# One order for all engines of an attention and soft-mixture layer: projections in pairs, contexts grouped, slot means in halves

## The chip, the cores and the metric

The kernel runs on one NeuronCore of a Trainium2 chip. The metric is the device time in microseconds (us) of one launch, the median over repeated runs. TensorE (PE) multiplies matrices, VectorE (DVE), ScalarE (ACT) and GpSimd (POOL) work on vectors, SyncE (SP) issues the transfers. Every engine works through its own list of instructions in order and waits on semaphores for the others.

## The reference

For each of 16 rows of the batch (256 tokens of 128 channels), with `xn = layernorm(x)`:

```
qkv = xn @ Wqkv + bqkv                      # 16 heads of 8 channels
proj = (q or k, each head scaled to length 1) @ omega   # 2 nodes x 32 features
feat = exp(clip(proj * sqrt(2s) - s, -20, 20)) / sqrt(32) * sqrt(weight)
attn = (causal sum of qf.kf * v) / (causal sum of qf.kf)
logits = rms_norm(xn) @ rms_norm(slots).T   # 512 slots
slots_in = softmax over experts of logits, applied to the tokens
hid = gelu(slots_in @ w1);  proc = hid @ w2
out = x + attn @ Wout + bout + softmax over slots of logits @ proc
```

## The kernel before, in words

**Tiling.** One row of the batch is one pass of `row(b, first, nxt, nxt2)`, and each engine has such a function with eight slots `s`. Slot `s` is built around `scores(b, s)`: the feature products of two heads (12 small matmuls, L925) into the PSUM tile `p_s`. DVE masks one half of it into `s_sb` (`evac_a`, L694), ACT copies the other (`evac_b`, L496), POOL masks that one (`mask_b`, L433). `run_rows` gives two rows out, a loop of two rows a turn, and two rows out.

**Features.** `project(b, g)` (L912) multiplies the turned stack of normalised q and k by omega, into `p_f` and `p_g`, each one bank; `clip(b, p)` (L688) moves one of them to `arg`, and `feature_exp(b, p)` (L491) makes `feat` for `scores(b, p)`. Four buffers of `arg` and of `feat` are there. `project(b, g)` waits for the clips of `g - 1`.

**The stack.** q and k of the next row (b1) pass through `qkv_product`, `qkv_bias`, `squares` (POOL, L404), `qk_norms`, `qk_root`, `qk_newton`, `qk_apply` (POOL, L419), `stack_high` (ACT, L484), `stack_low` (POOL, L427), and `turn_stack`, a transposing transfer from SP (L312) into `stack_t`. In `p_s` also stand the sums of `context` (L943).

**The slots.** Two logit products, their maxima (L720, L726), `shift`, the exponentials, `slot_sums` (L1012) into `x01`, `slots_norm` (a reciprocal and a product on DVE, L733 and L736), `slots_transposed` (L1021), `slots_high` and `slots_low`, two halves of `hidden` (L887), `gelu` (L523), two halves of `processed` (the product with w2, L1040), `proc_copy`, `combine` (L1051). What follows the hidden product of a row is done in slots 0 to 2 of the next row (bp is the row before).

**What sets the order.** It is written out by hand: the place of each call in the four `row` functions is the place of its instructions in the queue of that engine. The semaphores only hold an instruction back. `hold` is a wait with an empty instruction behind it.

Of the kernel before, what the change touches and what calls it, by code (L numbers as in the profile page):

```python
# [29 lines left out]
LN_EXP = "natural_log_exp_and_others"  # L30

# [53 lines left out]
def build(nc, x, Wqkv, bqkv, Wout, bout, omega, nodes, weights, gamma_x, gamma_slot, slot_embeds,  # L85
          w1, w2, out):
    with ExitStack() as ctx:
# [140 lines left out]
        stlo_ok = sem("stlo_ok")  # L228
        d_st = sem("d_st")
# [63 lines left out]
        def _(sp):  # L293
# [13 lines left out]
            def turn_stack(b):  # L307
                hold(sp, sthi_ok, count(b, 1, 1))
                hold(sp, stlo_ok, count(b, 1, 1))
                hold(sp, ft_ok, count(b, 4, -4))  # L310
# [53 lines left out]
        def _(pool):  # L364
# [70 lines left out]
            pool.wait_ge(d_bo, 16)  # L435
            residual((0, 0))
# [3 lines left out]
            place_v((0, 0))  # L440

# [18 lines left out]
        def _(act):  # L460
# [91 lines left out]
            ln_root(b1)  # L552
# [6 lines left out]
            stack_high(b0)  # L559
            act.wait_ge(se_cl, 1)  # L560
# [6 lines left out]
            feature_exp(b0, 0)  # L567

            def row(b, first, nxt, nxt2):

                b1, b2, bp = step(b, 1), step(b, 2), step(b, -1)
                for s in range(8):
                    if s == 0:
                        if not first:
                            ctx_copy(bp, 1)
                        feature_exp(b, 1)
                        if not first:
                            proc_copy(bp)
# [16 lines left out]
                    if s == 0 and nxt:  # L595
                        xt_high(b1)
                    if s == 4 and nxt:
                        stack_high(b1)
                    if s == 5 and nxt2:
                        ln_root(b2)  # L600
                    if s == 7:
# [3 lines left out]
                        if nxt:  # L605
                            feature_exp(b1, 0)
# [9 lines left out]
        def _(dve):  # L616
# [23 lines left out]
            def ln_apply(b):  # L640
# [3 lines left out]
                after(dve, sl_ok, count(b, 1, -1))  # L644
# [512 lines left out]
```

## Time and profile before

| | us |
|---|---|
| median of 3 runs (573.86 to 579.02) | 576.27 |
| the profiled execution | 578.53 |
| its span in the trace | 576.5 |
| PE busy | 484.0 (84%) |
| DVE busy | 348.8 (61%) |
| ACT busy | 322.6 (56%) |
| POOL busy | 174.1 (30%) |

A span is the time from the first to the last instruction in the trace; 2.0 us of the profiled execution lie outside it. Busy times of different engines overlap. An idle time stands in front of an instruction with the engine and the line that ended it.

### The profile page before, as it was taken

To read this page: it belongs to the slowest core of one execution; us is meant where nothing else is said; L and a number is where in the kernel's file an instruction comes from. 1 tells how busy PE (TensorE), PEld (TensorE's weight loads), DVE (VectorE), ACT (ScalarE), POOL (GpSimd) and SP (SyncE) were. 2 spreads that over 40 slices of the span, in tenths; PEclk is the share of its full clock that TensorE was granted. 3 is DMA by queue.
4 is the path that set the end of the run, shared out by engine and by line. 5 is a ranking of instruction groups with operands and counts; after the bars stand their busy time and mean duration, and the time that the engine had idled before them with its cause. 6 is when DMAs were issued, how large, how long until landed. Compare 5 with 4: busy or idle time off the path is not lost.

```text
span 576.5 us, 16010 instructions
## 1 busy us (share of the span) xinstructions
PE 484.0 (84%) x5768; PEld 394.3 (68%) x5768; DVE 348.8 (61%) x889; ACT 322.6 (56%) x560; POOL 174.1 (30%) x278
## 2 busy tenths in 40 slices
PE   4077998889799898979989897998989798898986
PEld 2056777768687676867767686776768677776866
DVE  3667484954748376574848647394775739484451
ACT  3237557455665647575564656656475655746562
POOL 4324141422414133231413324141332414233120
PEclk9999899979999799999989899898999989998999
DMA  2312002020200202020020202002020200102000
GB/s 71 75 24 48 1 11 47 10 48 2 53 5 9 45 9 45 0 55 0 9 45 9 45 0 50 5 9 45 9 45 0 55 0 9 38 11 38 3 9 9
DMA packets 45779, 14.46 MB, mean 25 GB/s; under 512 B 35640, under 2 KB 45624, under 8 KB 45752
## 3 DMA queue, kind: packets, MB, share of 16 engines
q1 hardware_dynamic: 45000, 13.80, 11.3%
q10 hardware_dynamic: 752, 0.30, 0.2%
q8 instruction: 17, 0.28, 0.2%
q14 instruction: 10, 0.08, 0.0%
HBM read 3.61 MB, written 2.10 MB: 10 GB/s over the span
## 4 chain that ended last, share of the span: by engine, by line
PE 53%; DMA 13%; DVE 13%; issue 9%; ACT 4%; POOL 4%; SPq 2%; DVEq 1%; POOLq 0%; ACTq 0%
PE x L887 15%; DMA stack_t<-stack 12%; PE x L1040 10%; PE p_s L925 9%; PE x L1051 5%; PE p_s L943 4%; DVE arg L688 4%; POOL stack L427 3%; DVE maxima L720 3%; PE p_f L912 2%; ACT stack L484 2%; DVE maxima L726 2%; PE x L966 2%; DVE small L672 2%; PE x L954 2%
## 5 line engine op out<-in xcount | busy, mean ns | idle before, releaser
L433 POOL TENSOR_TENSOR s_sb<-s_sb,causal 128x256 f32<-128x256 f32 x128 | 93.7, 732 | 306.9 <-ACT s_sb L496 306.9
L694 DVE TENSOR_TENSOR s_sb<-p_s,causal 128x384 f32<-128x384 f32 x128 | 70.6, 552 | 122.9 <-PE p_s L925 122.5
L925 PE MATMUL p_s<-feat 64*64 64x256 f32 (+3 forms) x2048 | 104.7, 322 | 10.3 <-ACT feat L491 6.2
L925 PEld LDWEIGHTS p_s<-feat 64*64 64x64 f32 x2048 | 82.8, 139 | 42.8 <-issue 33.4
L496 ACT ACTIVATE s_sb<-p_s 128x384 f32<-128x384 f32 x128 | 62.8, 490 | 85.2 <-PE p_s L925 84.9
L491 ACT ACTIVATE feat<-arg,f_bias 128x512 f32<-128x512 f32 x128 | 91.3, 714 | 0.2
L688 DVE TENSOR_SCALAR arg<-p_f,f_low,f_high 128x512 f32<-128x512 f32 x64 | 51.6, 806 | 26.1 <-PE p_f L912 26.1
L1040 PE MATMUL x<-w_sb,hid_t 128*128 128x128 f32 x512 | 64.0, 278 | 0.0
L1040 PEld LDWEIGHTS x<-w_sb,hid_t 128*128 128x128 f32 x512 | 60.8, 192 | 4.6 <-issue 3.2
L912 PE MATMUL p_f<-stack_t,omega_st 64*128 64x512 f16 x64 | 25.7, 402 | 41.4 <-DMA stack_t<-stack 41.4
L523 ACT ACTIVATE hid_t<-x 128x1024 f32<-128x1024 f32 x32 | 32.8, 1024 | 45.8 <-PE x L887 45.8
L943 PE MATMUL p_s<-s_sb,vw 128*32 128x128 f32 x1536 | 48.6, 274 | 6.7 <-DVE s_sb L694 6.7
L688 DVE TENSOR_SCALAR arg<-p_g,f_low,f_high 128x512 f32<-128x512 f32 x64 | 51.3, 801 | 0.0
L943 PEld LDWEIGHTS p_s<-s_sb,vw 128*32 128x32 f32 x1536 | 40.2, 110 | 13.1 <-DVE s_sb L694 11.2
L912 PEld LDWEIGHTS p_f<-stack_t,omega_st 64*128 64x128 f16 x64 | 6.0, 93 | 49.6 <-issue 46.4
L887 PE MATMUL x<-slot_hi,w_hi 128*128 128x512 f32 x64 | 34.0, 531 | 0.3 <-DVE slot_lo L741 0.3
L1012 PE MATMUL x<-xg,disp 128*128 128x129 f32 x256 | 32.8, 281 | 0.0
L1012 PEld LDWEIGHTS x<-xg,disp 128*128 128x128 f32 x256 | 29.8, 191 | 3.2 <-issue 3.2
L1051 PE MATMUL x<-proc,comb_t 128*128 128x129 f32 x256 | 31.4, 275 | 0.2 <-ACT proc L528 0.2
L1051 PEld LDWEIGHTS x<-proc,comb_t 128*128 128x128 f32 x256 | 30.7, 191 | 0.6 <-ACT proc L528 0.5
L887 PE MATMUL x<-slot_hi,w_lo 128*128 128x512 f32 x64 | 30.4, 476 | 0.0
L887 PE MATMUL x<-slot_lo,w_hi 128*128 128x512 f32 x64 | 30.3, 473 | 0.0
(131 smaller groups left out, 838.9 us busy)
## 6 DMA issues: line engine op xcount, KB each, us to landing
xin<-in_L_attn_x_dram SPq DMA_DIRECT2D x32, 64.0 KB, 2.4
out_dram<-out_sb SPq DMA_DIRECT2D x32, 64.0 KB, 2.1
se_rows<-n_L_ffn_slot_embeds_dram SPq DMA_DIRECT2D x1, 256.0 KB, 5.1
w_f<-in_L_ffn_w_dram SPq DMA_DIRECT2D x1, 256.0 KB, 5.3
w_sb<-in_L_ffn_w_dram SPq DMA_DIRECT2D x1, 256.0 KB, 4.7
stack_t<-stack SPq DMA_TRANSPOSE x16, 4.4
bqkv_bc<-in_L_attn_bqkv_dram ACTq DMA_DIRECT2D x1, 192.0 KB, 5.0
wqkv_f<-in_L_attn_Wqkv_dram SPq DMA_DIRECT2D x1, 192.0 KB, 4.9
```

Source lines behind the costliest of these rows:

```text
L433: pool.tensor_tensor(v, v, m, ALU.mult).then_inc(mb_ok, 1)
L491: nc.scalar.activation(feat[:, p % 4, :], arg[:, p % 4, :], ACT.Exp, bias=f_bias[:, 0:1]).then_inc(fe_ok, 1)
L496: nc.scalar.activation(s_sb[:, p, 1, :], p_s[:, 1, 0:384], ACT.Copy).then_inc(eb_ok, 1)
L688: nc.vector.tensor_scalar(arg[:, p % 4, :], bank[:, :], f_low[:, 0:1], f_high[:, 0:1], ALU.max, ALU.min).then_inc(cl_ok, 1)
L694: nc.vector.tensor_tensor(s_sb[:, p, 0, :], p_s[:, 0, 0:384], causal[:, :], ALU.mult).then_inc(ea_ok, 1)
L887: mm = nc.tensor.matmul(dst, a, w, start=start and i == 0, stop=stop and i == 2, skip_group_check=True)
L912: nc.tensor.matmul(bank[:, :], omega_st[rows, g, :], stack_t[rows, b[1], :, :, g, :].rearrange("p j k t -> p k j t"), start=True, stop=Tru ...
L925: mm = nc.tensor.matmul(p_s[rows:rows + 64, u, o:o + hi - lo], f[:, T + keys:T + keys + 64], f[:, lo:hi], start=True, stop=True, skip_grou ...
L943: mm = nc.tensor.matmul(p_s[32 * q:32 * q + 32, j, 384:512], vw[:, b[1], kt, QUADS * a + q, :], s_sb[:, p, q % 2, o:o + 128], start=(kt == ...
L1012: mm = nc.tensor.matmul(x01[:, half, 129 * (c % 2):129 * (c % 2) + 129], disp[:, j, 128 * c:128 * c + 128], xg[:, b[1], j, :], start=(j == ...
L1040: mm = nc.tensor.matmul(x01[:, 1, 128 * c:128 * c + 128], hid_t[:, m, 128 * c:128 * c + 128], w2_sb[:, m, :], start=(m == 0 and c == 0), s ...
L1051: mm = nc.tensor.matmul(x23[:, 0, 129 * j:129 * j + 129], comb_t[:, c, 128 * j:128 * j + 128], proc[:, c, :], start=(c == 0), stop=(c == N ...
```

## The change

The arithmetic stays; the order of calls on four engines changes, and three calls are split or moved.

- PE: `project(b, 0)` stands at the end of the row before, behind `scores(bp, 7)`, no longer ahead of the hidden products; `project(b, 1)` and `project(b, 2)` stand around the last contexts, ahead of `scores(b, 0)`. `project(b, 3)` is in slot 3 ahead of `shift`. `context(b, 0)` and `(b, 1)` go from slot 4 to slot 5, behind `slots_transposed`, both hidden products one slot forward.
- DVE: the clips follow the projections, so `clip(b, 4)` stands ahead of `evac_a(b, 0)` and three of them at the row's start; `ln_stats(b2)` moves from slot 4 to slot 0. `slots_norm` is two calls of half the size. `stack_again` is a new copy, float16 from SBUF to SBUF, of the part of the stack that ACT wrote twice before.
- ACT: one copy fewer in `stack_high`; the exponentials follow the clips; the table of the Gelu is loaded behind `ctx_copy(b, 0)`, no longer when the Gelu comes.
- SP: `turn_stack` also waits for the new copy.
- Before the rows: POOL's `residual((0, 0))`, with its wait for the bias, goes behind the work on the first stack; `project(b0, 0)` goes behind the transposes of the slot embeddings; the split of w1 on DVE goes into slot 1 of row 0.

Cut to its core:

```diff
@@ -432,12 +435,12 @@
 
-            pool.wait_ge(d_bo, 16)
-            residual((0, 0))
             squares((0, 0))
             qk_apply((0, 0))
             stack_low((0, 0))
             place_v((0, 0))
+            pool.wait_ge(d_bo, 16)
+            residual((0, 0))
@@ -480,9 +483,7 @@
                 after(act, d_st, count(b, 16, 0))
-                for q in (0, 2):
-                    last = nc.scalar.activation(stacked(q), parted(), ACT.Copy)
-                last.then_inc(sthi_ok, 1)
+                nc.scalar.activation(stacked(0), parted(), ACT.Copy).then_inc(sthi_ok, 1)
@@ -564,16 +565,19 @@
                 for s in range(8):
                     if s == 0:
+                        if nxt:
+                            xt_high(b1)
+                        feature_exp(b, 0)
                         if not first:
                             ctx_copy(bp, 1)
                         feature_exp(b, 1)
+                        feature_exp(b, 2)
                         if not first:
                             proc_copy(bp)
                     if s == 2 and not first:
@@ -582,28 +586,27 @@
                         qk_root(b1)
                     if s == 4:
                         dispatch_exp(b)
+                    evac_b(b, s)
+                    if s < 3:
+                        feature_exp(b, s + 3)
+                    if s == 1 and nxt2:
+                        ln_root(b2)
+                    if s == 4:
+                        if nxt:
+                            stack_high(b1)
+                        combine_exp(b)
+                        feature_exp(b, 6)
                     if s == 5:
+                        slots_high(b)
+                        feature_exp(b, 7)
                         ctx_copy(b, 0)
-                        combine_exp(b)
+                        nc.scalar.preload_act_table_set(GELU)
                     if s == 6:
-                        slots_high(b)
-                    if s == 7:
                         gelu(b, 0)
-                    evac_b(b, s)
-                    if 0 < s < 7:
-                        feature_exp(b, s + 1)
-                    if s == 0 and nxt:
-                        xt_high(b1)
-                    if s == 4 and nxt:
-                        stack_high(b1)
-                    if s == 5 and nxt2:
-                        ln_root(b2)
                     if s == 7:
                         gelu(b, 1)
                         if nxt:
                             nc.scalar.preload_act_table_set(LN_EXP)
-                        if nxt:
-                            feature_exp(b1, 0)
 
@@ -727,13 +730,17 @@
-            def slots_norm(b):
-                after(dve, sl_ok, count(b, 1, 1))
-                v = x01[:, :, 0:258].rearrange("p a (c d) -> p a c d", d=129)
-                nc.vector.reciprocal(slot_rs[:, :, :], v[:, :, :, C]).then_inc(slr_ok, 1)
-                after(dve, slr_ok, count(b, 1, 1))
-                rs = slot_rs[:, :, :].rearrange("p a (c d) -> p a c d", d=1).broadcast_to([128, 2, 2, C])
-                nc.vector.tensor_tensor(slot_v[:, :, :].rearrange("p (a c) d -> p a c d", a=2), v[:, :, :, 0:C], rs,
+            def stack_again(b):
+                after(dve, sthi_ok, count(b, 1, 1))
+                nc.vector.tensor_copy(stacked(2), stacked(0)).then_inc(stcp_ok, 1)
+
+            def slots_norm(b, half):
+                after(dve, sl_ok, count(b, 2, half + 1))
+                v = x01[:, half, 0:258].rearrange("p (c d) -> p c d", d=129)
+                nc.vector.reciprocal(slot_rs[:, half, :], v[:, :, C]).then_inc(slr_ok, 1)
+                after(dve, slr_ok, count(b, 2, half + 1))
+                rs = slot_rs[:, half, :].rearrange("p (c d) -> p c d", d=1).broadcast_to([128, 2, C])
+                nc.vector.tensor_tensor(slot_v[:, 2 * half:2 * half + 2, :], v[:, :, 0:C], rs,
                                         ALU.mult).then_inc(slv_ok, 1)
@@ -917,8 +934,8 @@
                 hold(pe, eb_ok, count(b, 8, p))
-                if p in (0, 5):
-                    hold(pe, cs_ok, count(b, 2, p // 5))
+                if p in (0, 6):
+                    hold(pe, cs_ok, count(b, 2, p // 6))
@@ -1061,31 +1077,36 @@
             qkv_product(b0)
-            pe.wait_ge(om_s, 3)
-            project(b0, 0)
             pe.wait_ge(se_ok, 1)
             pe.wait_ge(qkvs_ok, 1)
             for c in range(NCH):
                 mm = nc.tensor.transpose(x01[:, 0, 128 * c:128 * c + 128], se_n[:, c, :], ident[:, :])
             mm.then_inc(se_t, 1)
+            pe.wait_ge(om_s, 3)
+            project(b0, 0)
             pe.wait_ge(vz_const, 2)
             pe.wait_ge(se_l, 1)
 
             def row(b, first, nxt, nxt2):
                 b1, bp = step(b, 1), step(b, -1)
                 for s in range(8):
-                    if s == 0 and not first:
-                        processed(bp, 0)
-                        context(bp, 2)
-                        context(bp, 3)
-                        processed(bp, 1)
-                    scores(b, s)
                     if s == 0:
                         if not first:
-                            ctx_transposed(bp)
+                            processed(bp, 0)
                         if nxt:
                             transposes(b1)
                         project(b, 1)
+                        if not first:
+                            context(bp, 2)
+                            context(bp, 3)
+                            processed(bp, 1)
+                            project(b, 2)
+                    scores(b, s)
+                    if s == 0:
+                        if first:
+                            project(b, 2)
+                        else:
+                            ctx_transposed(bp)
                     if s == 1:
                         if nxt:
                             qkv_product(b1)
@@ -1098,25 +1119,23 @@
                             pe.wait_ge(d_late, 16 * LATE)
                         else:
                             attention_out(bp)
-                        project(b, 2)
                         logits_tokens(b, nxt)
                         logits_slots(b)
                     if s == 3:
+                        project(b, 3)
                         shift(b)
                     if s == 4:
-                        project(b, 3)
-                        context(b, 0)
-                        context(b, 1)
                         slot_sums(b, 0)
                         slot_sums(b, 1)
                     if s == 5:
                         slots_transposed(b)
+                        context(b, 0)
+                        context(b, 1)
+                        hidden(b, nxt, 0)
                     if s == 6:
-                        if nxt:
-                            project(b1, 0)
-                        hidden(b, nxt, 0)
-                    if s == 7:
                         hidden(b, nxt, 1)
+                    if s == 7 and nxt:
+                        project(b1, 0)
 
             run_rows(pe, row)
             last_row = (B // 2 - 1, 1)
```

The new `row` of DVE (its old one is above):

```
def row(b, first, nxt, nxt2):
    b1, b2, bp = step(b, 1), step(b, 2), step(b, -1)
    for s in range(8):
        if s == 0:
            clip(b, 2)
            if nxt:
                xt_low(b1)
            clip(b, 3)
            if not first:
                if nxt2:
                    ln_stats(b2)
                clip(b, 4)
        if s == 2 and not first:
            add_experts(bp)
        if s == 3:
            token_maxima(b)
            slot_maxima(b)
        evac_a(b, s)
        if s == 0:
            if first:
                clip(b, 4)
                ln_stats(b2)
            clip(b, 5)
        if s == 1:
            if first:
...
            else:
                ctx_norm(bp)
            if nxt:
                qkv_bias(b1)
        if s == 2:
            if not first:
                add_attention(bp)
            if nxt:
                qk_norms(b1)
        if s == 3 and nxt:
            qk_newton(b1)
        if s == 4:
            clip(b, 6)
            slots_norm(b, 0)
            if nxt:
                stack_again(b1)
            slots_norm(b, 1)
        if s == 5:
            clip(b, 7)
            slots_low(b)
        if s == 6 and nxt2:
            ln_apply(b2)
        if s == 7 and nxt:
            clip(b1, 0)
            clip(b1, 1)
```

Three places of the order. First PE, from the last scores of one row to the first scores of the next. In the kernel before (`w_sb,hid_t` is `processed`, `s_sb,vw` is `context`, `ident,xg` the transposes of the next row's input):

```order
L1040 MATMUL x<-w_sb,hid_t 128x128 x8
L943 MATMUL p_s<-s_sb,vw 32x128 x24
L1040 MATMUL x<-w_sb,hid_t 128x128 x8
L925 MATMUL p_s<-feat 64x256 x2
L925 MATMUL p_s<-feat 64x192 x2
L925 MATMUL p_s<-feat 64x64 x2
L925 MATMUL p_s<-feat 64x128 x2
L954 MATMUL x<-ident,ctx_sb 128x128 x4
L895 MATMUL x<-ident,xg 128x128 x2
L912 MATMUL p_f<-stack_t,omega_st 128x512
L912 MATMUL p_g<-stack_t,omega_st 128x512
```

And in the changed kernel:

```order
L929 MATMUL p_f<-stack_t,omega_st 128x512
L929 MATMUL p_g<-stack_t,omega_st 128x512
L1056 MATMUL x<-w_sb,hid_t 128x128 x8
L912 MATMUL x<-ident,xg 128x128 x2
L929 MATMUL p_f<-stack_t,omega_st 128x512
L929 MATMUL p_g<-stack_t,omega_st 128x512
L960 MATMUL p_s<-s_sb,vw 32x128 x24
L1056 MATMUL x<-w_sb,hid_t 128x128 x8
L929 MATMUL p_f<-stack_t,omega_st 128x512
L929 MATMUL p_g<-stack_t,omega_st 128x512
L942 MATMUL p_s<-feat 64x256 x2
```

Three pairs of projections now stand between the two scores, where one pair stood behind the first scores.

Second PE, from the transposes of the slot means to the hidden product. Before:

```order
L1021 MATMUL x<-ident,slot_v 128x128 x4
L925 MATMUL p_s<-feat 64x256 x2
L925 MATMUL p_s<-feat 64x192 x2
L925 MATMUL p_s<-feat 64x64 x2
L925 MATMUL p_s<-feat 64x128 x2
L912 MATMUL p_f<-stack_t,omega_st 128x512
L912 MATMUL p_g<-stack_t,omega_st 128x512
L887 MATMUL x<-slot_hi,w_hi 128x512
```

Changed:

```order
L1037 MATMUL x<-ident,slot_v 128x128 x4
L960 MATMUL p_s<-s_sb,vw 32x128 x24
L904 MATMUL x<-slot_hi,w_hi 128x512
L904 MATMUL x<-slot_lo,w_hi 128x512
L904 MATMUL x<-slot_hi,w_lo 128x512
```

The next row's projection is gone from here, and the contexts have come in.

Third DVE, slots 4 and 5. Before:

```order
L694 TENSOR_TENSOR s_sb<-p_s,causal 128x384
L688 TENSOR_SCALAR arg<-p_f,f_low,f_high 128x512
L630 BN_STATS bn<-xin 128x6 x2
L634 BN_AGGR mv<-bn 128x2 x2
L637 TENSOR_SCALAR small<-mv 128x2
L638 TENSOR_SCALAR small<-mv 128x2
L688 TENSOR_SCALAR arg<-p_g,f_low,f_high 128x512
L733 RECIPROCAL slot_rs<-x 128x4
L736 TENSOR_TENSOR slot_v<-x,slot_rs 128x512
L694 TENSOR_TENSOR s_sb<-p_s,causal 128x384
L741 TENSOR_TENSOR slot_lo<-x,slot_hi 128x512
```

Changed:

```order
L697 TENSOR_TENSOR s_sb<-p_s,causal 128x384
L691 TENSOR_SCALAR arg<-p_f,f_low,f_high 128x512
L740 RECIPROCAL slot_rs<-x 128x2
L743 TENSOR_TENSOR slot_v<-x,slot_rs 128x256
L735 COPY stack<-stack 128x32x16
L740 RECIPROCAL slot_rs<-x 128x2
L743 TENSOR_TENSOR slot_v<-x,slot_rs 128x256
L697 TENSOR_TENSOR s_sb<-p_s,causal 128x384
L691 TENSOR_SCALAR arg<-p_g,f_low,f_high 128x512
L748 TENSOR_TENSOR slot_lo<-x,slot_hi 128x512
```

The statistics are gone, the slot means come in halves, and the new copy stands between the halves.

## Rows read from the trace of the kernel before

**Rows 1.** Page: busy time, TensorE clock, chain, transfers.

```profile
PE 484.0 (84%) x5768; PEld 394.3 (68%) x5768; DVE 348.8 (61%) x889; ACT 322.6 (56%) x560; POOL 174.1 (30%) x278
...
PEclk9999899979999799999989899898999989998999
...
PE 53%; DMA 13%; DVE 13%; issue 9%; ACT 4%; POOL 4%; SPq 2%; DVEq 1%; POOLq 0%; ACTq 0%
...
stack_t<-stack SPq DMA_TRANSPOSE x16, 4.4
```

**Rows 2.** Chain that ended last: start us, us, what.

```profile
65.72 1.98 PE x L1040 x16
...
537.04 1.98 PE x L1040 x16
...
566.66 2.00 PE x L1040 x16
```

**Rows 3.** Timeline, PE, one row: start us, us, engine line op [idle before].

```profile
340.63 0.44 PE L887 MATMUL x<-wqkv_hi,xt_hi 128*128 128x384 f32 x1 [0.60 <-DVE xt_lo L657]
...
349.79 0.62 PE L996 MATMUL x<-neg_ident,maxima 128*128 128x128 bf16 x8 [0.45 <-DVE maxima L726]
...
351.01 0.77 PE L925 MATMUL p_s<-feat 64*64 64x256 f32 x16 [0.17 <-issue]
...
352.54 1.52 PE L943 MATMUL p_s<-s_sb,vw 128*32 128x128 f32 x48 [0.43 <-DVE s_sb L694]
...
357.04 0.66 PE L1021 MATMUL x<-ident,slot_v 128*128 128x128 f32 x4 [0.30 <-DVE slot_v L736]
358.08 0.77 PE L925 MATMUL p_s<-feat 64*64 64x256 f32 x16 [0.38 <-ACT feat L491]
360.29 0.37 PE L912 MATMUL p_f<-stack_t,omega_st 64*128 64x512 f16 x1 [1.43 <-DMA stack_t<-stack]
```

**Rows 4.** Windows: stretch us, length, busy PE PEld DVE ACT POOL, PEclk, DMA share, GB/s.

```profile
348.90:349.90 1.00, 0.55 (x18) 0.40 (x11) 1.00 (x3) 0.47 (x2) 0.00 (x0) 1.00 0.00 0
...
359.90:360.90 1.00, 0.61 (x3) 0.42 (x4) 0.14 (x2) 0.98 (x2) 0.40 (x1) 1.00 0.34 100
...
361.90:362.90 1.00, 1.00 (x3) 0.44 (x2) 0.95 (x5) 0.00 (x0) 0.00 (x0) 0.50 0.00 0
```

**Rows 5.** Timeline, PE: hidden products and scores behind, middle row and last row.

```profile
360.61 0.50 PE L887 MATMUL x<-slot_hi,w_hi 128*128 128x512 f32 x1
...
363.08 1.34 PE L925 MATMUL p_s<-feat 64*64 64x256 f32 x16
...
559.47 0.49 PE L887 MATMUL x<-slot_hi,w_hi 128*128 128x512 f32 x1 [0.35 <-DVE slot_lo L741]
...
561.07 0.78 PE L925 MATMUL p_s<-feat 64*64 64x256 f32 x16
```

**Rows 6.** Timeline, other engines of that row.

```profile
352.95 1.14 ACT L484 ACTIVATE stack<-qk_n 128x512 f16<-128x512 f32 x2
...
354.04 0.81 DVE L688 TENSOR_SCALAR arg<-p_g,f_low,f_high 128x512 f32<-128x512 f32 x1
...
354.35 1.16 POOL L427 TENSOR_TENSOR stack<-qk_n,stack 128x512 f16<-128x512 f32 x1 [0.87 <-ACT stack L484]
...
356.30 0.69 DVE L736 TENSOR_TENSOR slot_v<-x,slot_rs 128x512 f32<-128x512 f32 x1
...
367.16 1.28 ACT L604 ACT_TABLE_LOAD   x1
```

**Rows 7.** Timeline, POOL and DVE before the first row.

```profile
13.51 0.62 DVE L666 SCALAR_TENSOR_TENSOR qkv<-x,small,bqkv_bc 128x384 f32<-128x384 f32 x1 [0.26 <-PE x L887]
...
17.53 0.72 POOL L398 TENSOR_TENSOR xres<-xin,bout_bc 128x256 f32<-128x256 f32 x1 [10.72 <-DMA bout_bc<-in_L_attn_bout_dram]
...
24.64 1.26 POOL L427 TENSOR_TENSOR stack<-qk_n,stack 128x512 f16<-128x512 f32 x1 [1.39 <-ACT stack L484]
24.80 1.12 DVE L807 TENSOR_SCALAR small<-small 128x4 f32<-128x4 f32 x1
```

More of the change, by code:

```diff
@@ L30 @@
 LN_EXP = "natural_log_exp_and_others"
+GELU = "gelu_and_others"
 def count(b, per, extra):
@@ L799, in _ @@
             last.then_inc(om_s, 1)
+            stack_again(b0)
+            ln_stats(b1)
             dve.wait_ge(f_ln, 1)
@@ L836, in row @@
                 for s in range(8):
-                    if s == 1 and nxt:
-                        xt_low(b1)
-                    if s == 2 and nxt:
-                        qkv_bias(b1)
+                    if s == 0:
+                        clip(b, 2)
+                        if nxt:
+                            xt_low(b1)
+                        clip(b, 3)
+                        if not first:
+                            if nxt2:
+                                ln_stats(b2)
+                            clip(b, 4)
+                    if s == 2 and not first:
+                        add_experts(bp)
                     if s == 3:
@@ L843, in row @@
                         slot_maxima(b)
-                    if s == 6:
-                        slots_low(b)
-                    if s == 1:
-                        clip(b, 3)
-                    if s == 3:
-                        clip(b, 5)
+                    evac_a(b, s)
+                    if s == 0:
+                        if first:
+                            clip(b, 4)
+                            ln_stats(b2)
+                        clip(b, 5)
+                    if s == 1:
+                        if first:
+                            dve.wait_ge(d_w1, 32)
+                            nc.vector.tensor_scalar(w1_hi[:, :], w1_f[:, :], gx_col[:, 0:1], None, ALU.mult).then_inc(w1_split, 1)
+                            dve.wait_ge(w1_split, 1)
+                            nc.vector.scalar_tensor_tensor(w1_lo[:, :], w1_f[:, :], gx_col[:, 0:1], w1_hi[:, :].bitcast(F32), ALU.mult,
+                                                       ALU.subtract).then_inc(w1_split, 1)
+                        else:
+                            ctx_norm(bp)
+                        if nxt:
+                            qkv_bias(b1)
@@ new lines, in row @@
+                    if s == 2:
+                        if not first:
+                            add_attention(bp)
+                        if nxt:
+                            qk_norms(b1)
+                    if s == 3 and nxt:
+                        qk_newton(b1)
+                    if s == 4:
+                        clip(b, 6)
+                        slots_norm(b, 0)
+                        if nxt:
+                            stack_again(b1)
+                        slots_norm(b, 1)
@@ L850, in row @@
                     if s == 5:
                         clip(b, 7)
-                        slots_norm(b)
-                    if s == 7 and nxt:
-                        clip(b1, 1)
-                    if s == 2 and not first:
-                        add_experts(bp)
-                    evac_a(b, s)
-                    if s == 1 and not first:
-                        ctx_norm(bp)
-                    if s == 2 and not first:
-                        add_attention(bp)
-                    if s in (0, 2, 4):
-                        clip(b, s + 2)
@@ L1088, in row @@
                         project(b, 1)
+                        if not first:
+                            context(bp, 2)
[3 more added lines that the diff above has]
+                    scores(b, s)
+                    if s == 0:
+                        if first:
+                            project(b, 2)
+                        else:
+                            ctx_transposed(bp)
                     if s == 1:
```

32 lines of the change are left out of this document (11 added, 21 removed).

## The prediction

> **What bounds the kernel now.** I read the page first [rows 1]: PE is busy for 84% of the span and has over half of the chain, no other engine is above 61%. The slices of the PE clock hold 7s and 8s again and again. So there are two things to gain: time in which PE stands, and time in which it runs slowly.
>
> The chain gives the length of a row [rows 2]. The second half of the w2 product (L1040) closes a row's work on the slots. It starts at 65.72 for row 0, at 537.04 for row 14 and at 566.66 for row 15: 471.32 / 14 = 33.67 us a row, 29.62 for the last one, which prepares no next row, and from there 576.5 - 566.66 = 9.8 to the end.
>
> The timeline of PE for one middle row shows its seven waits [rows 3]: 0.60 (xt_lo), 0.45 (maxima), 0.17 (issue), 0.43 (contexts, for the masked scores), 0.30 (slot means), 0.38 (feature) and 1.43 (the transposing transfer), 3.76 together. After the longest one the windows [rows 4] show the granted clock at 0.50, which is 1.2 GHz, where it had been 1.00 (2.4 GHz). What that costs is read by comparing the same instructions [rows 5]: first half of the hidden product 363.08 - 360.61 = 2.47, in the last row, which has no such transfer, 561.07 - 559.47 = 1.60; scores behind it 1.34 against 0.78. That is 0.87 + 0.56 = 1.4 us. So of 33.7 us PE needs 33.7 - 3.8 - 1.4 = 28.5 at the full clock, and 5.2 are open.
>
> **The change, wait by wait.** PE's instructions are the same in number and size, so I keep 28.5 and ask of each wait what is in front of it now. I lay the new order out from the first `project(b, 0)`, at the start of a row's period (0), with the durations of this trace; the times are estimates.
>
> *The transfer, 1.43 and its clock, 1.4.* Its chain is unchanged in length but for ACT, which copies the stack once and not twice (1.14 for two [rows 6], so 0.6 less). `stack_low` on POOL (1.16 [rows 6]) ends at about 21.5, the transfer is issued behind it and lands 4.4 later [rows 1], near 26.3. `project(b1, 0)`, which stood ahead of both hidden halves, now stands behind them and two scores, at 28.5 or later. Some 2 us of cover: the wait goes, and the slow stretch with it. If the cover is gone, each us late is paid in full, and the clock's 1.4 comes back.
>
> *xt_lo, 0.60.* `transposes(b1)` now stands two projections, two contexts, half the w2 product and two scores ahead of `qkv_product`, over 6 us of PE work where 1.4 stood. Gone. At the front ACT must still pass the Gelu, the table (1.28 [rows 6]), `xt_high` and one exponential: done near 3.8, scores(b, 0) come at 6.6.
>
> *maxima, 0.45, and issue, 0.17.* `project(b, 3)`, 0.3 of work, fills the wait ahead of `shift`, and the clip that DVE did behind the maxima is gone from there, so `evac_a(b, 3)` comes 0.7 earlier. Both gone.
>
> *contexts, 0.43.* They wait for the evacuation of the scores ahead of them; the transposes of the slot means, 0.66 [rows 3], stand between now. Gone.
>
> *feature, 0.38.* `feature_exp(b, 6)` and `(b, 7)` stand ahead of the evacuations that used to delay them. Gone.
>
> *slot means, 0.30.* Here I expect a loss. In halves, only the second half (half of 0.69 [rows 6], and its reciprocal, about 0.55) is left when the slot sums end, against scores of 0.7 on PE: by itself the wait would fall to 0.15. But `stack_again` stands between the halves, and ACT's copy releases it and POOL's `stack_low` at the same moment. The trace shows what such a pair does [rows 7]: a DVE operation on 4 elements a partition issued at 24.80, while POOL's `stack_low` ran from 24.64 to 25.90, took 1.12 us and ended with it. So the copy will end with POOL's 1.16, not after the 0.2 to 0.8 of a DVE copy of 512 elements (a clip of that size takes 0.81 [rows 6]; the trace has no float16 copy). I take 0.5 for it, giving a wait of 0.65; the bounds are 0 and 1.1.
>
> The Trainium skill (SBUF — State Buffer, Who interferes with whom) says that such a copy and a GpSimd instruction share a pair of ports, and that the one issued first holds it to its end. This trace shows the case with POOL first; if DVE came first, by that rule the copy would pass and only `stack_low` would start some 0.3 later, inside the transfer's cover. By POOL first the sum is as below, by DVE first it is 15 x 0.5 = 7.5 us less.
>
> *New: scores(b, 1) for `evac_a(b, 0)`.* `clip(b, 4)` now stands in front of it and starts only when the projection just ahead of the scores is done: 0.4 + 0.7 (clip) + 0.5 (evacuation) against 0.3 + 0.7 + 0.6 of PE work. With a semaphore's way, 0.15.
>
> Sum of a row: 28.5 + 0.65 + 0.15 = 29.3, which saves 4.4.
>
> *Before the rows.* POOL waited 10.72 us for a bias that only `residual` needs, and the squares behind it started at 18.2 [rows 7], though DVE's q and k were there at 14.1 [rows 7]. Now they start there, ACT copies once, and DVE's statistics of row 1 stand behind: the first transfer starts 4.2 earlier. But the slot embeddings' chain on DVE, now 3.6 earlier, ends last before the first projection; then `scores(b0, 0)` waits for `xt_high` and an exponential, and row 0 takes up a clip, the statistics of row 2 and the split of w1 ahead of `qkv_bias`, about 1.5. I keep 2.1, bounds 0 and 4.2. The rest of row 0 saves 4.0 as any row's second part does.
>
> *The last row* is 29.3 less the copy's 0.5 and less what is there for a next row (two projections 0.6, transposes 0.3, the q, k, v product 1.2): 26.7, which saves 2.9. The end, 9.8, is unchanged.
>
> Sum on the profiled execution: 576.5 - 2.1 - 4.0 - 14 x 4.4 - 2.9 = 505.9 of span, 2.0 outside it, 507.9. That execution, 578.5, is 2.3 above the median shown, so 505.6: **506 us**, 12% less. Its own range, 497 to 515, is 4.2 of doubt in the head and the copy at 0 or at 1.1.
>
> **The rivals.**
>
> *A: small waits take the place of the seven.* I counted two and took every other chain as fitting. DVE is the fullest of the others, and from `clip(b, 4)` to `qkv_bias` it has 5 us without a break beside as much PE work. For it: each order has its own waits, and the one before has seven. Against: DVE has 348.8 / 16 = 21.8 us of work in a row of 29 [rows 1]. 1 us more a row: 506 + 15 = 521. Chance 0.20.
>
> *B: the clock still falls.* The wait for the slot means would start it. Against: in the row before, PE was busy 0.55 of a us at 348.9 and the clock stayed at 1.00; it fell after 1.43 idle behind two shorter waits [rows 3, 4]. 15 x 1.4: 527. Chance 0.08.
>
> *C: the transfer is still late.* `stack_low` can be held by the copy, and the transfer waits for both. It would need 2 us; a late us with the clock's part costs 15 x 2.4: 542. Chance 0.06.
>
> *D: slower than before.* The place is between `scores(b, 4)` and the hidden product: slot sums, means in halves, transposes, contexts, each waiting for another engine, with no projection among them. If PE's waits there add up so that the clock stays at 1.2 GHz through half the row, PE's 14 us of that half take up to 28. A slow stretch costs 1.4 here; it decides once four such stretches stand in a row (5.6 against the 4.4 saved): 15 x 1.2 = 18 above 576, 594. Nothing in the rows shows more than one. Chance 0.03.
>
> *E: the change does nothing.* All seven waits come back elsewhere, as when two chains are both one row long. 576. Against: PE's sum is 28.5 and no chain crosses the row's end with less than about 2 us to spare. Chance 0.02.
>
> **How the numbers follow.** The forecast has 0.61, A 0.20, B 0.08, C 0.06, D 0.03, E 0.02. The range goes from 494, where no wait at all is left (15 x 0.8 less), to 528, which takes in A and B and leaves out C to E and the unlikely ends, 0.15 together. About 1% is what a measurement tells from no change. Faster by more: all but D and E, 0.95; within 1%: 0.02; slower: 0.03.
>
> **What would show it.** In the profile after: rows 29.3 long between the starts of the second w2 product; no DMA in front of the projection and a PE clock of 1.00 from the first row to the last; a wait of 0.5 to 0.8 in front of the transposes of the slot means, and the copy on DVE ending with POOL's `stack_low`; PE busy near 484 - 15 x 1.4 = 463, 92% of the span. Wrong it would be if a wait above 0.3 stands elsewhere in each row, most likely in front of scores 1 or of the hidden product, or if the slices of the clock still show 8s.

## The result, and the profile after

The changed kernel takes **509.19 us** in the median of 4 runs (508.64 to 510.51), the kernel before 575.55 (573.86 to 579.02): 0.8844 of the time, 95% interval 0.8797 to 0.889. The forecast was 506. The profiled execution took 508.64, its span is 506.6 (forecast 505.9).

The page of the changed kernel, beside [rows 1]: busy times, clock slices, chain.

```profile
PE 462.0 (91%) x5768; PEld 377.2 (74%) x5768; DVE 376.6 (74%) x937; ACT 312.4 (62%) x544; POOL 175.0 (35%) x278
...
PEclk9559999999999999999999999999999999999999
...
PE 74%; DVE 17%; issue 6%; ACTq 1%; ACT 1%; DVEq 0%; POOL 0%; POOLq 0%
```

PE is 22 us less busy with the same 5768 instructions: 1.4 a row of slow clock, gone. The 7s and 8s of the clock line are gone behind the head (its two 5s are taken up in the last section), and DMA is gone from the chain. DVE is 27.8 busier: 6.1 is the new copy, 4.9 the halves of the slot means, and 16 are three small instructions that now run beside POOL's (last section): two of the norms of q and k, and one of the layer norm of a later row.

The chain of the changed kernel (start us, us, what), beside [rows 2]: the second half of the w2 product for rows 0, 14 and 15. L1056 is L1040 of before.

```profile
60.62 1.98 PE x L1056 x16
...
469.87 1.98 PE x L1056 x16
...
496.77 2.00 PE x L1056 x16
```

A row is (469.87 - 60.62) / 14 = 29.23 us, the last one 26.90, the end 9.83. Row 0 arrives 5.1 earlier. So 5.1 + 14 x 4.43 + 2.7 = 69.9, the difference of the spans.

PE's timeline in a middle row, beside [rows 3] (start us, us, engine, line, operation, [idle before]):

```profile
337.28 0.62 PE L1013 MATMUL x<-neg_ident,maxima 128*128 128x128 bf16 x8 [0.21 <-DVE maxima L729]
...
341.79 0.66 PE L1037 MATMUL x<-ident,slot_v 128*128 128x128 f32 x4
342.77 1.52 PE L960 MATMUL p_s<-s_sb,vw 128*32 128x128 f32 x48 [0.33 <-DVE s_sb L697]
...
348.83 0.39 PE L929 MATMUL p_f<-stack_t,omega_st 64*128 64x512 f16 x1
...
357.11 0.77 PE L942 MATMUL p_s<-feat 64*64 64x256 f32 x16 [0.33 <-DVE s_sb L697]
```

Seven waits of 3.76 have become three of 0.87. None is left ahead of the slot means (L1037), where I had forecast 0.65, nor ahead of the next row's projection (L929 at 348.83). Two are other than forecast: 0.33 ahead of the contexts (L960), which I had put at 0, and 0.33 ahead of scores 1, which I had put at 0.15. Summed over the launch (PE's waits: us in total, times, longest):

```profile
PE x L1083 <- DVE se_n L827: 13.5, 1, 13.5
PE p_s L960 <- DVE s_sb L697: 5.1, 14, 0.4
PE p_s L942 <- DVE s_sb L697: 5.0, 16, 0.3
...
PE x L1013 <- DVE maxima L729: 2.0, 7, 0.8
```

The engine named ahead of the contexts is not the one that ended the wait. ACT's timeline there:

```profile
340.68 1.01 ACT L516 ACTIVATE comb_t<-x 128x1024 f32<-128x1024 f32 x1
341.58 0.71 ACT L492 ACTIVATE feat<-arg,f_bias 128x512 f32<-128x512 f32 x1
342.20 0.48 ACT L497 ACTIVATE s_sb<-p_s 128x384 f32<-128x384 f32 x1
```

The evacuation `evac_b` (L497) ends at 342.68, 0.09 before the contexts start; DVE's part had ended at 342.38. It stood behind `combine_exp` and `feature_exp(b, 6)`. `combine_exp` stood ahead of this evacuation before too; what the change did is to put `feature_exp(b, 6)` there, and to make the contexts wait for this evacuation, of scores 5, where in slot 4 they had waited for that of scores 4.

### The profile page after: what moved, and what is told of

Read it like the earlier page. It is cut to its first block, busy times and chain, and to the rows that moved or that the text cites. A ratio compares the mean times of both kernels' runs of the same rounds, so it can differ in the third digit from the quotient of the medians.

```text
span 506.6 us, 16039 instructions
## 1 busy us (share of the span) xinstructions
PE 462.0 (91%) x5768; PEld 377.2 (74%) x5768; DVE 376.6 (74%) x937; ACT 312.4 (62%) x544; POOL 175.0 (35%) x278
## 4 chain that ended last, share of the span: by engine, by line
PE 74%; DVE 17%; issue 6%; ACTq 1%; ACT 1%; DVEq 0%; POOL 0%; POOLq 0%
PE x L904 14%; PE p_s L942 14%; PE x L1056 13%; PE p_s L960 9%; PE x L1029 6%; PE x L1067 6%; PE p_f L929 3%; DVE maxima L723 3%; DVE maxima L729 3%; PE x L983 2%; PE x L1037 2%; DVE arg L691 2%; PE x L1013 2%; DVE small L675 2%; DVE s_sb L697 2%
## 5 line engine op out<-in xcount | busy, mean ns | idle before, releaser
L497 ACT ACTIVATE s_sb<-p_s 128x384 f32<-128x384 f32 x128 | 62.7, 490 | 77.2 <-PE p_s L942 77.1
L942 PEld LDWEIGHTS p_s<-feat 64*64 64x64 f32 x2048 | 78.6, 133 | 38.3 <-issue 30.2
L942 PE MATMUL p_s<-feat 64*64 64x256 f32 (+3 forms) x2048 | 100.2, 311 | 5.9 <-DVE s_sb L697 5.0
L492 ACT ACTIVATE feat<-arg,f_bias 128x512 f32<-128x512 f32 x128 | 89.7, 714 | 0.1
L1056 PE MATMUL x<-w_sb,hid_t 128*128 128x128 f32 x512 | 65.7, 281 | 0.0
L1056 PEld LDWEIGHTS x<-w_sb,hid_t 128*128 128x128 f32 x512 | 59.6, 191 | 6.6 <-issue 6.6
L960 PE MATMUL p_s<-s_sb,vw 128*32 128x128 f32 x1536 | 48.6, 274 | 5.1 <-DVE s_sb L697 5.1
L960 PEld LDWEIGHTS p_s<-s_sb,vw 128*32 128x32 f32 x1536 | 40.4, 110 | 12.3 <-DVE s_sb L697 8.4
L904 PE MATMUL x<-slot_hi,w_hi 128*128 128x512 f32 x64 | 28.6, 447 | 0.0
L407 POOL TENSOR_TENSOR qk_sq<-qkv 128x512 f32<-128x512 f32 x16 | 16.7, 1044 | 31.7 <-DVE qkv L669 31.7
L929 PE MATMUL p_f<-stack_t,omega_st 64*128 64x512 f16 x64 | 25.4, 396 | 0.0
L929 PE MATMUL p_g<-stack_t,omega_st 64*128 64x512 f16 x64 | 25.4, 397 | 0.0
L904 PE MATMUL x<-slot_hi,w_lo 128*128 128x512 f32 x64 | 25.4, 397 | 0.0
```

Source lines behind the costliest of these rows:

```text
L492: nc.scalar.activation(feat[:, p % 4, :], arg[:, p % 4, :], ACT.Exp, bias=f_bias[:, 0:1]).then_inc(fe_ok, 1)
L497: nc.scalar.activation(s_sb[:, p, 1, :], p_s[:, 1, 0:384], ACT.Copy).then_inc(eb_ok, 1)
L904: mm = nc.tensor.matmul(dst, a, w, start=start and i == 0, stop=stop and i == 2, skip_group_check=True)
L929: nc.tensor.matmul(bank[:, :], omega_st[rows, g, :], stack_t[rows, b[1], :, :, g, :].rearrange("p j k t -> p k j t"), start=True, stop=Tru ...
L942: mm = nc.tensor.matmul(p_s[rows:rows + 64, u, o:o + hi - lo], f[:, T + keys:T + keys + 64], f[:, lo:hi], start=True, stop=True, skip_grou ...
L960: mm = nc.tensor.matmul(p_s[32 * q:32 * q + 32, j, 384:512], vw[:, b[1], kt, QUADS * a + q, :], s_sb[:, p, q % 2, o:o + 128], start=(kt == ...
```

## The experiments

Lines with - are the changed kernel's, with + the experiment's, unless said otherwise; the edits are shortened to the calls that matter. Ratios are to the kernel before in the same session.

**The one call.** Everything of the change, but the next row's projection back at its old place.

```diff
                         context(b, 1)
+                        if nxt:
+                            project(b1, 0)
                         hidden(b, nxt, 0)
                     if s == 6:
                         hidden(b, nxt, 1)
-                    if s == 7 and nxt:
-                        project(b1, 0)
```

> The changed kernel with one call put back: the next row's first projection stands ahead of both hidden halves again. Theory (the gain needs the cover of the transposing transfer): in a middle row of the changed kernel the transfer is issued at 342.74 and lands 4.4 later, PE would reach the projection at 344.2, so it waits about 3.2 us, and the granted clock falls to 0.50 behind it for another 1.4: rows of 32.4 to 33.8, 554 to 573 us. Rival (the cover is worth only the wait that the kernel before had there): rows of 30.7, 529 us, clock at 1.00.

Measured: **580.48 us** (579.99 to 583.36), ratio 1.0178 (1.0057 to 1.0299), rows of (537.38 - 66.99) / 14 = 33.60. PE's timeline:

```profile
361.11 0.37 PE L929 MATMUL p_f<-stack_t,omega_st 64*128 64x512 f16 x1 [2.80 <-DMA stack_t<-stack]
...
361.44 0.79 PE L904 MATMUL x<-slot_hi,w_hi 128*128 128x512 f32 x1
...
364.29 1.03 PE L942 MATMUL p_s<-feat 64*64 64x256 f32 x16
365.25 0.50 PE L904 MATMUL x<-slot_hi,w_hi 128*128 128x512 f32 x1
```

And one of its windows, as in [rows 4], with the granted clock at 0.50:

```profile
362.00:363.00 1.00, 1.00 (x4) 0.78 (x3) 0.00 (x0) 0.00 (x0) 0.00 (x0) 0.50 0.00 0
```

The wait is 2.80, twice what it was, since in the new order PE reaches this projection sooner after the transfer's issue; the first half behind it takes 364.29 - 361.44 = 2.85 where it needs 1.60, its scores 0.96 where 0.70 is the rule. 3.0 of wait (45.4 in 15 rows) and 1.5 of slow clock take all 4.4 of a row's gain back. The time is above what I expected. All the other moves together, with this one call left where it was, gain nothing: the kernel is 0.6 to 3% slower than the one before in its own session, and that one has medians of up to 579.08 in other sessions, so how much slower is not settled.

The same call alone, in the order of before (lines are the kernel before's):

```diff
                     if s == 6:
-                        if nxt:
-                            project(b1, 0)
                         hidden(b, nxt, 0)
                     if s == 7:
+                        if nxt:
+                            project(b1, 0)
                         hidden(b, nxt, 1)
```

(DVE's `clip(b1, 0)` and `clip(b1, 1)` follow to the end of its row.)

> The kernel before with one move alone: the next row's first projection stands behind scores 7, ahead of the second hidden half, and its two clips at the end of DVE's row. Theory: the 1.43 us wait for the transfer and most of the 1.4 us of slow clock go, small waits stay: rows of 31.0 to 31.4 in place of 33.67, 537 to 545 us. Rival (the clips and the first exponential of the next row come late and the next scores wait instead): no change, 576.

Measured: **546.76 us** (545.98 to 548.11), ratio 0.9568 (0.9463 to 0.9673), a little above what I expected. The windows of two rows (stretch us, length, busy PE PEld DVE ACT POOL, granted clock, DMA share, GB/s) and PE's waits:

```profile
101.95:133.58 31.63, 28.55 (x363) 23.58 (x362) 21.48 (x55) 19.82 (x34) 10.53 (x16) 1.00 0.13 27
133.58:165.15 31.57, 28.55 (x363) 23.60 (x362) 21.33 (x54) 19.73 (x34) 10.52 (x16) 1.00 0.13 26
```

```profile
PE p_f L911 <- DMA stack_t<-stack: 18.6, 1, 18.6
PE x L886 <- DVE slot_lo L741: 10.2, 16, 0.7
PE x L886 <- DVE xt_lo L657: 9.4, 15, 1.0
PE x L995 <- DVE maxima L726: 7.7, 16, 0.7
PE p_s L942 <- DVE s_sb L694: 6.7, 16, 0.4
PE p_s L924 <- ACT feat L491: 6.2, 16, 0.4
PE x L1020 <- DVE slot_v L736: 4.8, 16, 0.3
```

The transfer's wait is left only ahead of row 0, and the clock stays at 1.00. But the projection had also covered the way to `slot_lo`: with it gone, the hidden product waits 0.64 a row, a wait that before did not show. The other five shown are still here as in [rows 3]. These six come to 45.0. In their place the whole change has 14.5 (12.1 in the three waits above, 2.4 in row 0), and 5.1 less ahead of row 0 (18.6 to 13.5): 35.6 of the 38.6 between the spans, 545.2 and 506.6. The rest I leave open.

**The contexts' wait.** ACT's queue or the transposes' length? First, ACT copies the stack twice again in the changed kernel, and DVE's copy is gone.

```diff
-                nc.scalar.activation(stacked(0), parted(), ACT.Copy).then_inc(sthi_ok, 1)
+                for q in (0, 2):
+                    last = nc.scalar.activation(stacked(q), parted(), ACT.Copy)
+                last.then_inc(sthi_ok, 1)
```

> The changed kernel with both stack copies on ACT again and none on DVE. Theory: the contexts of slot 5 wait for ACT's evacuation of scores 5, which stands behind this copy in ACT's queue; 0.5 us more there makes that wait 0.33 + 0.5, rows of 29.7, 514 to 518 us. Rival (DVE's masked half is what the contexts wait for, as the profile names it): the copy's going frees DVE, rows of 29.0 to 29.2, 506 to 509.

Measured: **515.01 us** (514.79 to 515.72), ratio 0.902 (0.8921 to 0.9118). The contexts' wait (L958 here):

```profile
PE p_s L958 <- DVE s_sb L698: 12.6, 15, 0.9
```

It is 0.84 a row for 0.36: 0.48 more, for a copy that lengthens ACT's queue by 0.52 (1.15 for two, 0.63 for one). It is ACT's queue. So take something out of it: `feature_exp(b, 6)` behind the evacuation.

```diff
                         combine_exp(b)
-                        feature_exp(b, 6)
                     if s == 5:
                         slots_high(b)
+                        feature_exp(b, 6)
```

> The changed kernel with feature exponential 6 behind ACT's evacuation of scores 5 and slots_high, no longer ahead of them. Theory (ACT's queue is what the contexts wait for): the 0.33 us goes to under 0.1, rows of 28.9 to 29.0, 504 to 506 us. Rival (DVE's masked half, as the profile names it): no change, 509.

Measured: **504.67 us** (504.01 to 505.41), ratio 0.8744 (0.8703 to 0.8785). The contexts now follow the transposes without a gap, on PE's timeline:

```profile
339.85 0.66 PE L1037 MATMUL x<-ident,slot_v 128*128 128x128 f32 x4
340.52 1.52 PE L960 MATMUL p_s<-s_sb,vw 128*32 128x128 f32 x48
```

In two rows a wait for the transfer now shows ahead of the projection, 0.7 together.

**The maxima.** POOL's `place_v` ahead of `residual`, so that the residual no longer runs beside DVE's limits and reductions.

```diff
+                        place_v(b1)
                         residual(b1)
-                        place_v(b1)
```

> The changed kernel with place_v ahead of residual on POOL alone. Theory: the clamp of the head norms on DVE takes 0.2 in place of 0.47 us, the maxima come 0.2 earlier, the wait ahead of the shift goes to 0: rows of 29.0, 506 us. Rival (the clamp then waits for a piece of place_v): no change, 509.

Measured: **506.54 us** (505.72 to 506.63); the changed kernel has 509.2 to 509.4 in its own sessions. DVE's clamp of the head norms (L678) falls from 0.44 to 0.24 in the mean. The maxima's 2.0 are gone, and the contexts' wait is 3.5 in 14 rows, 0.25 for 0.36.

**Slot means in halves, and the copy between them.** The means whole again, one reciprocal and one product behind both slot sums:

```diff
-                        slots_norm(b, 0)
                         if nxt:
                             stack_again(b1)
-                        slots_norm(b, 1)
+                        slots_norm(b)
```

> The changed kernel with the slot means in one piece on DVE, the stack copy ahead of them. Theory: the transposes of the slot means wait about 0.25 us more, but the contexts behind them wait for ACT in any case, so that wait shrinks by as much: rows of 29.2 to 29.4, 509 to 511 us. Rival (the halves carry gain of their own, as the forecast had it): 0.4 more a row, 515 us.

Measured: **509.57 us** (508.63 to 509.76), ratio 0.8918 (0.882 to 0.9016), no change. 0.30 a row stands ahead of the transposes again (4.8 in 16), and the contexts' wait behind it is gone: one replaces the other. So in this kernel the halves win nothing; whether they would with ACT's evacuation out of the way was not tried. Then the copy behind both halves, so that POOL starts first:

```diff
                         slots_norm(b, 0)
+                        slots_norm(b, 1)
                         if nxt:
                             stack_again(b1)
-                        slots_norm(b, 1)
```

> The changed kernel with the stack copy on DVE behind the second half of the slot means, so that it is issued some 0.5 us after POOL's stack_low has begun. Theory (the one issued first holds the other off): the copy takes 0.8 to 1.0 us in place of 0.28 and ends with stack_low, evac_a(b, 5) comes after it, the contexts wait 0.7 in place of 0.33, rows of 29.6, 513 to 516 us. Rival (they don't hinder each other): copy 0.28, rows of 29.2, 509.

Measured: **510.38 us** (510.09 to 512.49). The copy and POOL's instruction, in the changed kernel:

```profile
340.91 0.28 DVE L735 COPY stack<-stack 128x512 f16<-128x512 f16 x1
```

```profile
341.10 1.17 POOL L430 TENSOR_TENSOR stack<-qk_n,stack 128x512 f16<-128x512 f32 x1 [0.38 <-ACT stack L486]
```

and in the experiment:

```profile
343.00 0.76 DVE L735 COPY stack<-stack 128x512 f16<-128x512 f16 x1
```

```profile
342.44 1.16 POOL L430 TENSOR_TENSOR stack<-qk_n,stack 128x512 f16<-128x512 f32 x1 [0.38 <-ACT stack L486]
```

With DVE first the copy takes 0.28. With POOL first it takes 0.76 and ends 0.16 behind POOL. The median of the 16 copies goes from 289 to 761 ns. It costs less than I expected, the contexts' wait growing from 0.36 to 0.48 (6.8 in 14 rows), since ACT's evacuation covers most of it.

**Scores 1.** First the place of the clip: `clip(b, 4)` behind the mask.

```diff
                                 ln_stats(b2)
-                            clip(b, 4)
...
                     evac_a(b, s)
                     if s == 0:
+                        clip(b, 4)
                         if first:
-                            clip(b, 4)
                             ln_stats(b2)
```

> The changed kernel with clip 4 behind the masked evacuation of scores 0 on DVE. Theory: scores 1 wait only for ACT's copy, 0.33 us goes to about 0.1, rows of 29.0, 505 to 507 us. Rival (ACT's copy ends no earlier): no change, 509.

Measured: **509.54 us** (509.12 to 510.51), ratio 0.8834. The wait stands at 5.0 in 16 rows: my theory of it fell. In the changed kernel, scores 0 start at 355.42 on PE, DVE masks one part of them and ACT copies the other:

```profile
356.34 0.55 DVE L697 TENSOR_TENSOR s_sb<-p_s,causal 128x384 f32<-128x384 f32 x1
356.37 0.49 ACT L497 ACTIVATE s_sb<-p_s 128x384 f32<-128x384 f32 x1 [0.57 <-PE p_s L942]
```

They end within 0.03 of each other, at 356.89 and 356.86, and scores 1 start at 357.11. With the clip behind the mask the same two end at 357.27 and 357.24 and scores 1 start at 357.49, behind scores 0 at 355.80: no time is saved, since the clip had ended in time. So what holds scores 1 is not the clip in DVE's queue but the length of the way through the evacuation itself. It is as long on both engines, and no run here tells which of them ends the wait. PE has only 0.66 of other work in between, where before it had the input's transposes and a projection as well.

The three moves together (`feature_exp(b, 6)`, `place_v`, `clip(b, 4)`):

> The changed kernel with both edits, and on POOL place_v ahead of residual, so that the clamp of the head norms on DVE (0.47 us beside residual, 0.20 without) doesn't hold the maxima. Theory: three waits of 0.33, 0.33 and 0.21 go to 0.1 together, rows of 28.5 to 28.7, 498 to 501 us. Rival (each wait taken away shows another of its size behind): 505 to 509.

Measured: **503.14 us** (502.55 to 503.95), ratio 0.8719 (0.8678 to 0.876). That is 6.2 less, not the 8 or more that I expected, since the clip's move had done nothing. Of the waits that come in every row only the one ahead of scores 1 is left (4.9 in 16); one of 0.74 for the transfer stands in one row. So to the same kernel a fourth move, work between scores 0 and 1:

```diff
                             processed(bp, 1)
-                            project(b, 2)
                     scores(b, s)
                     if s == 0:
-                        if first:
-                            project(b, 2)
-                        else:
+                        project(b, 2)
+                        if not first:
                             ctx_transposed(bp)
```

> The changed kernel with the three moves of the run before it (503.14 us) and a fourth: the projection of the third pair of pieces is called behind scores 0 of each row instead of ahead of them, so that 0.32 us of projection and 0.66 us of context transposes lie between scores 0 and scores 1. Theory: what is left of the wait ahead of scores 1 (0.3 us a row) is ScalarE's copy of scores 0, 0.49 us and its way, about 1.0 us from the end of the product that it reads; with 0.98 us of work between, the wait is gone: rows of 28.3 to 28.4 us, 498 to 500 us. Rival: the projection only changes its place and the wait comes back ahead of scores 0 or of the features, since what these read is then late by the same 0.3 us: 503 us.

Measured: **498.53 us** (497.44 to 499.18), ratio 0.8638 (0.8597 to 0.8679), 2% faster than the changed kernel. PE's timeline where the gap was:

```profile
346.48 0.77 PE L941 MATMUL p_s<-feat 64*64 64x256 f32 x16
347.18 0.39 PE L928 MATMUL p_f<-stack_t,omega_st 64*128 64x512 f16 x1
...
347.50 0.66 PE L970 MATMUL x<-ident,ctx_sb 128*128 128x128 f32 x4
348.17 0.77 PE L941 MATMUL p_s<-feat 64*64 64x256 f32 x16
```

And the marks of the chain, rows 0 and 14:

```profile
59.64 1.98 PE x L1055 x16
...
458.15 1.98 PE x L1055 x16
```

28.46 us a row, with one wait of PE, 0.18 for a transfer, between these two marks: what is left is the 28.5 of PE's own work that the forecast started from.

**The work before the rows.** In the kernel before, only POOL's `residual` and its wait moved:

```diff
-            pool.wait_ge(d_bo, 16)
-            residual((0, 0))
             squares((0, 0))
...
+            pool.wait_ge(d_bo, 16)
+            residual((0, 0))
```

> The kernel before with one edit: POOL's first residual, with its wait for the bias, behind the work on the first stack. Theory: the first projection comes about 4 us earlier (27.5 in place of 31.5) and all behind it too, as the old order has no clip, statistics or w1 split ahead of the first bias: 3.5 to 4 us less, 571 to 572 where the kernel before has 575. Rival (the slot embeddings then end last): 1 to 2 us less.

Measured: **572.9 us** (571.4 to 573.38); the kernel before in that session 579.08 in the median of 7, but from 562.19 to 580.43, so its ratio is not given. The execution of 562.19 has a mean granted clock of 0.990, the other six have 0.934 to 0.961; it seems that the slow stretches cost less in some executions of the kernel before, and part of what any ratio to it says is this. The span is 569.5 for 576.5, and the first wait for the transfer 13.6 for 18.0. Of the 7.0 that is 4.4; waits for the later transfers are 1.2 less (35.8 - 13.6 against 41.4 - 18.0), and the rest I leave open. The whole is more than the 3.5 to 4 that I expected.

The changed kernel once more, beside other experiments:

> The changed kernel once more, as the measure for the three beside it: 509 us, rows of 29.2.

Measured: **509.37 us** (508.97 to 510.02), ratio 0.8828 (0.8786 to 0.8869).

## Why the prediction was right, step by step

- **The frame, 28.5 of PE work a row:** right. The fourth move brings the row to 28.46 with hardly a wait left.
- **Transfer 1.43 and its clock 1.4, gone:** right, and larger than its own terms suggest. The transfer is issued at 342.74, lands some 4.4 later near 347.1, and the projection starts at 348.83: 1.7 of cover where I said 2. It is thin: the slowest of the 16 transfers lands in 5.6, and in the experiments with shorter rows PE waits for one, by up to 0.74. That the transfer's wait brings the slow clock is shown from both sides, by the move alone (clock 1.00) and by the one call put back (0.50 again).
- **xt_lo 0.60, issue 0.17, feature 0.38, gone:** right, none of them shows in a middle row.
- **Maxima 0.45, gone:** half right; 2.0 in 7 rows are left. I had counted DVE's queue but not what runs beside it on POOL.
- **Contexts 0.43, gone:** wrong, 0.33 is left. I said that the transposes' 0.66 would cover the evacuation and looked at PE's side alone; on ACT 1.0 + 0.6 stand in front of the evacuation that the contexts now wait for, and the 0.6, `feature_exp(b, 6)`, is there by the change. Moved behind it, it is worth 4.7 us.
- **Slot means 0.30 to 0.65:** wrong in the middle rows, where the wait is 0. The copy starts 0.19 before POOL's `stack_low` and takes 0.28. The case that I took as the rule is there in row 0, where POOL started first: copy 0.91 from 48.09, POOL 1.16 from 47.68, and PE waited 0.62 for the means. I had read who is released together, not who gets there first. The other branch of the prediction, "by DVE first", 7.5 us less, is what happened at this place.
- **Scores 1, 0.15:** the place right, the size 0.33, and the cause half wrong: the clip that I priced into it ends in time, and the way through DVE's mask or ACT's copy is as long without it.
- **A row, 29.3:** 29.23. That it came so close is partly luck. Over all rows the contexts' wait is 5.1 / 14 = 0.36, that of scores 1 is 5.0 / 16 = 0.31 or 0.16 over mine, the maxima's 2.0 / 14 = 0.14: 0.66 too little, against 0.65 too much at the means.
- **Its own signs:** PE busy (463 forecast, 462.0 measured), a clock of 1.00 through the rows and no transfer in front of the projection came. The wait ahead of the slot means and a copy ending with POOL's `stack_low` did not, and one sign of being wrong did: waits above 0.3 stand elsewhere in each row, ahead of scores 1 and of the contexts. And the narrow range has a slip: 2.1 for the head and 15 x 0.5 below, 15 x 0.6 above give 496 to 517, not 497 to 515.
- **The head, 2.1:** logits of row 0 begin at 39.61 for 41.46 before, 1.85 less. The transfer starts at 21.07 for 25.98 but the slot embeddings end last, as forecast: 13.5 of wait for `se_n`. The rest of row 0 saved 3.2, not 4.0, with the copy's 0.62 and a wait for the maxima of 0.8 in it.
- **Last row 2.9, end 9.8:** 2.7 and 9.83.
- **Rivals.** A has its signs, but the three small waits come to 0.81 a row where I had counted 0.80. B and C did not come: clock 1.00 through the rows, 1.7 of cover. D's time, no gain or a loss, is what the first experiment makes of the change by one call, but by the mechanism of C (transfer late, then slow clock), not by the one I gave for D. E fell with the result.

## What to carry to other kernels

When an order of one engine is laid out anew, go through every wait on both sides: what lies between producer and consumer on the waiting engine, and what was put in front of the producer on its own. A call that leaves too little cover for a transfer's whole way, such as a projection that comes before the hidden products, can outweigh all the others. Its price depends on what stands around it: moving this call was worth about 25 us in the old order (0.9568 of 575 to 579), where it moved past one hidden half and one scores, and 71 in the new one (580.48 to 509.37), where it moved past two of each. And when a row's period is the work of one engine plus its waits, filler between two dependent products can be worth as much as it is long: 0.32 of projection took away a wait of 0.33, 4.6 us in all, and with the two moves in the other engines' queues a row went from 29.23 to 28.46.

## What the runs showed of the hardware

**Who comes first at the shared port pair.** A copy of 128x512 float16 between SBUF buffers took 0.28 us with DVE first and 0.76 with POOL's instruction first. The Trainium skill (SBUF — State Buffer, Who interferes with whom) says that the engine which issues first holds the pair for its whole instruction and the other waits. The order with POOL first agrees. With DVE first the copy is not held, as it says, but POOL is hardly seen to wait: its instruction takes 1.17 when it starts 0.19 behind the copy, 1.16 in the experiment where it comes first, and at most 1.29 where, in the experiment with `place_v` first, it starts 0.01 behind: a hold of 0.13 at most, for a copy of 0.28. The same section of the Trainium skill also says that a DVE instruction with two inputs in SBUF contends with a GpSimd instruction that reads SBUF, and even a small one shows it, on DVE's and POOL's timelines of the changed kernel:

```profile
337.61 0.68 DVE L623 SCALAR_TENSOR_TENSOR small<-small 128x64 f32<-128x64 f32 x1
338.32 0.22 DVE L625 TENSOR_TENSOR small<-small 128x64 f32<-128x64 f32 x1
```

```profile
337.48 0.73 POOL L436 TENSOR_TENSOR s_sb<-s_sb,causal 128x256 f32<-128x256 f32 x1 [1.92 <-ACT s_sb L497]
```

64 elements a partition take 0.68 beside POOL's mask and end 0.08 behind it; the next instruction of that size takes 0.22.

**The recorded clock ahead of the first row.** The windows give 0.52 for 26 to 36 us in the changed kernel and 1.00 for the same stretch of the kernel with whole means. The first scores took 1.34 us in both, and in the kernel before too, whose record says 1.00 there as well; in the rows, at 1.00, they take 0.77. Behind a long idle stretch I would trust the durations rather than the record.
